# State copies behind the scans moved from ScalarE to VectorE in a Mamba-and-FFN block

## The reference

```python
mod = (_silu(c) @ wmod).reshape(1, 6, 1, -1)            # sa, ca, ga, sb, cb, gb
h = layernorm(x) * (1 + ca) + sa
# selective scan, D_INNER 1024, D_STATE 16
dt = softplus(dt_in @ dt_proj.T + bias);  dA = exp(dt * A);  dBx = dt * B * h
def step(hs, (dA_t, dBx_t, C_t)):  hs = dA_t * hs + dBx_t;  y = sum_n hs[., n] * C_t[n]
x = x + ga * (y + D * h)
h = layernorm(x) * (1 + cb) + sb
# FFN 1024 -> 2752 -> 1024, gate/up/down each with a rank-16 addition, silu(gate) * up
x = x + gb * ffn(h)
```

## Time and profile before

| | us |
|---|---|
| median of 3 runs | 2325.9 (2323.68 to 2330.59) |
| profiled execution | 2327.44 |
| its span, first to last instruction | 2325.6 |
| TensorE busy | 2064.8 |
| GpSimd busy | 1543.6 |
| VectorE busy | 1444.6 |
| ScalarE busy | 1061.0 |
| mean granted TensorE clock | 0.939 of full speed |

### The profile page before, as it was taken

One profiled execution on the slowest core, in us unless ns is written; L12 is line 12 of the kernel. 1 busy time (PEld: TensorE's weight loads), 2 busy tenths in 40 slices (PEclk: granted clock), 3 DMA queues, 4 the chain that ended last, 5 costly groups with the idle time before them and its releaser, 6 DMA issues.

```text
span 2325.6 us, 33254 instructions
## 1 busy us (share of the span) xinstructions
PE 2064.8 (89%) x11700; PEld 1875.5 (81%) x11700; DVE 1444.6 (62%) x2119; ACT 1061.0 (46%) x2378; POOL 1543.6 (66%) x960
## 2 busy tenths in 40 slices
PE   7577765878788999999999989999989999999999
PEld 4233324767777988888999989999889999999999
DVE  4664667667756778867778767778757774211111
ACT  3776766565535555544555444545444332310000
POOL 1477768997887797868877867867859896110100
PEclk9797867889888999999999999999999999999999
DMA  9799774777868677767577666677677877787786
GB/s 359 287 348 350 258 285 157 265 251 271 298 215 306 227 254 249 282 216 272 200 264 249 223 227 255 221 252 258 219 226 261 276 248 272 245 298 264 254 291 221
DMA packets 121205, 603.01 MB, mean 259 GB/s; under 512 B 10576, under 2 KB 23120, under 8 KB 80464
## 3 DMA queue, kind: packets, MB, share of 16 engines
q1 hardware_dynamic: 121040, 600.89, 73.4%
HBM read 514.63 MB, written 86.21 MB: 258 GB/s over the span
## 4 chain that ended last, share of the span: by engine, by line
PE 59%; DVE 14%; ACT 8%; issue 8%; POOL 6%; DMA 3%; DVEq 0%; ACTq 0%; SPq 0%; POOLq 0%
PE FP L759 50%; DVE ring L1162 6%; PE FP L647 4%; DVE ring L1047 3%; POOL ring L1276 2%; DVE FP L1137 2%; ACT SC L830 1%; ACT sqb L947 1%; PE FP L783 1%; DMA raw<-w_gu 1%; PE FP L720 1%; PE FP L676 1%; POOL y L1251 1%; DMA wts<-w_scratch 1%; POOL xlo L1267 1%
## 5 line engine op out<-in xcount | busy, mean ns | idle before, releaser
L759 PE MATMUL FP<-xhi,wts 128*128 128x368 f32 (+2 forms) x4320 | 1079.3, 326 | 76.8 <-issue 28.0
L759 PEld LDWEIGHTS FP<-xhi,wts 128*128 128x128 f32 x4320 | 774.8, 194 | 86.8 <-issue 78.3
L1276 POOL TENSOR_TENSOR ring<-ring,c_row 128x736 f32<-128x736 f32 (+2 forms) x372 | 621.2, 1670 | 295.6 <-ACT hst L847 295.1
L830 ACT ACTIVATE SC<-dtb,aneg 128x368 f32<-128x368 f32 (+2 forms) x768 | 412.1, 545 | 730.7 <-DVE ring L1162 729.5
L759 PE MATMUL FP<-xlo,wts 128*128 128x368 f32 (+2 forms) x2160 | 700.4, 324 | 0.0
L759 PE MATMUL FP<-hhi,wts 128*128 128x368 f32 (+5 forms) x2376 | 574.3, 323 | 39.8 <-POOL hlo L1291 22.9
L1162 DVE TENSOR_TENSOR_SCAN ring<-SC,hst,ring 128x368 f32<-128x368 f32 (+1 forms) x640 | 579.7, 947 | 3.1 <-ACT SC L830 3.1
L1251 POOL TENSOR_TENSOR y<-y,ring 128x736 f32<-128x736 f32 (+1 forms) x320 | 554.7, 1733 | 13.7
L759 PEld LDWEIGHTS FP<-hhi,wts 128*128 128x128 f32 (+1 forms) x2376 | 410.5, 187 | 47.0 <-POOL hlo L1291 23.6
L759 PEld LDWEIGHTS FP<-xlo,wts 128*128 128x128 f32 x2160 | 419.3, 194 | 1.1
L1047 DVE TENSOR_TENSOR ring<-hb,SC 128x736 f32<-128x736 f32 (+2 forms) x384 | 328.2, 855 | 102.2 <-PE FP L676 76.6
(11 more groups left out here) (102 smaller groups left out, 1966.9 us busy)
## 6 DMA issues: line engine op xcount, KB each, us to landing
wts<-w_scratch SPq DMA_DIRECT2D x249, 1152.0 KB, 5.3
wts<-w_scratch SPq DMA_DIRECT2D x91, 896.0 KB, 5.0
wts<-w_scratch SPq DMA_DIRECT2D x51, 1024.0 KB, 5.4
w_scratch<-wts SPq DMA_DIRECT2D x44, 1152.0 KB, 7.4
raw<-w_gu SPq DMA_DIRECT2D x44, 576.0 KB, 6.3
modw<-mod_w SPq DMA_DIRECT2D x24, 1024.0 KB, 11.0
w_scratch<-wts SPq DMA_DIRECT2D x16, 896.0 KB, 6.4
w_scratch<-wts SPq DMA_DIRECT2D x9, 1024.0 KB, 5.2
```

The source lines that it names most:

```text
L759: last = mm(out, w, x, start=(start and k == 0 and e == 0), stop=(stop and k == n - 1 and e == 2))
L830: A(decays(c, n, a), tile_of(dtb, c, i), ACT.Exp, scale=aneg[:, i * NS + s:i * NS + s + 1]).then_inc(a_da[a], 1)
L1276: G.tensor_tensor(buf, buf, over_pair(c_of(k)), ALU.mult).then_inc(g_hc, 1)
```

## The change

`keep_state` leaves ScalarE's list and stands in VectorE's, directly behind the two scans of the group, as a `tensor_copy` with the semaphore `v_save`. It waits for both scans. In the last chunk, whose states nobody reads, there is no copy, and GpSimd waits for the scans instead. The scans of a chunk's first pair wait for `v_save` where they waited for `a_save`.

```diff
--- before.py
+++ after.py
@@ -384,7 +384,7 @@
         a_xs, a_part, a_sp, a_fac = sem("xs_rounded"), sem("abs_ready"), sem("exp_ready"), sem("factor_ready")
         a_ini, a_keep = sem("h_times_d_ready"), sem("dt_kept")
         a_da = [sem(f"decay{a}_ready") for a in range(2)]
-        a_bc, a_save = sem("c_copied"), sem("state_kept")
+        a_bc, v_save = sem("c_copied"), sem("state_kept")
         a_hi, a_ts, a_th, a_hh = sem("weight_hi_ready"), sem("lora_rounded"), sem("tanh_ready"), sem("hidden_hi_ready")
 
         v_const, v_c, v_mod, v_modstep, v_late = sem("vector_const_ready"), sem("silu_c"), sem("mod_ready"), sem("mod_step"), sem("mod_cols_copied")
@@ -838,13 +838,6 @@
                 elif k >= C_FIRST:
                     act.wait_ge(g_hc, k - C_FIRST + 1)
                 A(c_of(k), SC[:, BC0 + k % 2, 0:CH[row_state(k)[0]]], ACT.Copy).then_inc(a_bc, 1)
-
-            def keep_state(c, n):
-                T = CH[c]
-                s, q = state_of(c, n)
-                for a in range(2):
-                    act.wait_ge(v_scan[a], group_id(c, n) + 1)
-                A(hst[:, s * ND + 2 * q:s * ND + 2 * q + 2], ring_of(c, n)[:, :, T - 1], ACT.Copy).then_inc(a_save, 1)
 
             def hi_part(u, hi, src):
                 w = raw_cols(u)
@@ -963,7 +956,6 @@
                             decay(0, n + 2)
                         elif n + 2 > GROUPS:
                             decay(1, 0)
-                        keep_state(0, n)
                         if n + 3 <= GROUPS:
                             copy_c(n + 3)
                     else:
@@ -971,7 +963,6 @@
                             copy_c(row_id(c, n) + 1)
                         if group_after(c, n):
                             decay(*group_after(c, n))
-                        keep_state(c, n)
 
             def split_hi(g):
                 k = OTF.index(g)
@@ -1045,6 +1036,12 @@
                 dve.wait_ge(pe_b, k + 1)
                 ring_free(dve, c, n)
                 V.tensor_tensor(ring_of(c, n), pair_of(hb, c, q), over_pair(SC[:, BC0 + k % 2, 0:T]), ALU.mult).then_inc(v_dbx, 1)
+
+            def keep_state(c, n):
+                s, q = state_of(c, n)
+                for a in range(2):
+                    dve.wait_ge(v_scan[a], group_id(c, n) + 1)
+                V.tensor_copy(hst[:, s * ND + 2 * q:s * ND + 2 * q + 2], ring_of(c, n)[:, :, CH[c] - 1]).then_inc(v_save, 1)
 
             def mod_vectors(n):
                 step = [{0: 0, 1: 1, 2: 5}[n]]
@@ -1152,7 +1149,7 @@
                         dbx(*group_after(c, n))
                     dve.wait_ge(v_dbx, g + 1)
                     if c and q == 0:
-                        dve.wait_ge(a_save, 3 * NS + s + 1 if c == 1 else group_id(c - 1, n) + PAIRS)
+                        dve.wait_ge(v_save, 3 * NS + s + 1 if c == 1 else group_id(c - 1, n) + PAIRS)
                     for a in range(2):
                         i = 2 * q + a
                         buf = ring_of(c, n)[:, a, :]
@@ -1161,6 +1158,8 @@
                             dve.wait_ge(a_da[1], g + 1)
                         V.tensor_tensor_scan(buf, decays(c, n, a), buf, hst[:, s * ND + i:s * ND + i + 1] if c else 0.0,
                                              ALU.mult, ALU.add).then_inc(v_scan[a], 1)
+                    if c + 1 < CHUNKS:
+                        keep_state(c, n)
                 elif kind == "evac":
                     q, T = p[1], CH[0]
                     dve.wait_ge(pe_y, NS * (q + 1))
@@ -1272,7 +1271,11 @@
                     if group_id(c, n) > GROUPS:
                         add(*divmod(group_id(c, n) - 1, GROUPS))
                     pool.wait_ge(a_bc, k + 1)
-                    pool.wait_ge(a_save, group_id(c, n) + 1)
+                    if c + 1 < CHUNKS:
+                        pool.wait_ge(v_save, group_id(c, n) + 1)
+                    else:
+                        for a in range(2):
+                            pool.wait_ge(v_scan[a], group_id(c, n) + 1)
                     G.tensor_tensor(buf, buf, over_pair(c_of(k)), ALU.mult).then_inc(g_hc, 1)
                     if not group_after(c, n):
                         add(c, n)
```

## The result

The changed kernel takes 2356.17 us (median of 6 runs, 2353.03 to 2359.1) against 2325.9: ratio 1.0129, 95% interval 1.0114 to 1.0145, so about 30 us slower, where 2354 had been forecast. The profiled execution took 2353.03 us, the shortest of the six, so the two profiles lie 25.6 us apart and not 30; its span is 2351.2, the mean granted clock 0.934 (0.939 before).

A forecast was written before the change was run, and what follows sets the result against it. TensorE was busy 2064.8 of 2325.6 us, so other engines matter only where it stands. Terms -8.0, -8.3, +11.5, +7.7 and +25 gave +28 us, 2354 us; own range 2328 to 2380 (58%), over all cases 2314 to 2390.

The forecast's parts named there:

- The deciding term: VectorE's copy behind the scans is held while GpSimd's instruction runs: 0.55 us left in the mean over 318 scan ends.
- ScalarE -8.0: Copies leaving ScalarE: 80 places on the chain at 0.10 us each, 8.0 us less.
- GpSimd -8.3: GpSimd's multiply by C starts earlier, after VectorE's copy: 15 places on the chain at 0.55 us, 8.3 us less.
- The unheld copy: VectorE's cost per copy when nothing blocks it: 0.03 us wait, 0.135 us copy, lost overlap; together 0.25 us.
- the first rival: The tiny VectorE copy isn't held by GpSimd: -2 us, 2324 us, no measurable change; chance 18%.
- The three positive terms: Losses in the sum: VectorE's 25 chain places +11.5, GpSimd's wait for the copy +7.7, copies off the chain +25 us.
- the term for the 25 places: Where the chain goes from a group's second scan to another VectorE instruction: 25 x (0.25 + 0.21) = +11.5 us.
- the coarse term for the other 143: Off the chain, 143 groups pushed by 0.79 us each, 112 us, times 0.225 = +25 us; ends 0 and 50.
- GpSimd's new wait: GpSimd, busy at the scans' end, then waits for a copy starting only when it pauses: 25 x 0.31 = +7.7 us.
- The coarse share: VectorE's time on the chain, 326 us of its 1444.6 us busy: 0.225, applied to delays off the chain.
- Place: Predicted profile sign: TensorE's lost time grows between 383 and 1645 us, its busy time doesn't.
- The third rival: VectorE's copy is passed over while GpSimd has a further instruction ready: +34 beside the +28 us, 2388 us; chance 10%.

The follow-up runs named there:

- Two pairs of kernels: tensor_copy against tensor_reduce on VectorE: in the changed kernel 1.0129 and 1.0002; as an additional instruction in the kernel before 1.0177 and 1.0051.
- the last chunk's edit: Kernel before, with ScalarE's copies left out in the last chunk alone, where GpSimd waits for the scans: 2326.25 us, ratio 0.9988.
- the reduce: Changed kernel with a tensor_reduce (max over one element) in place of each tensor_copy on VectorE: 2329.12 us, ratio to before 1.0002.
- the extra reduce: Kernel before, ScalarE's copies kept, plus a VectorE tensor_reduce into a spare buffer behind the scans, GpSimd waiting for both: 2338.15 us, 1.0051.
- the extra copy: Kernel before, ScalarE's copies kept, plus a VectorE tensor_copy into a spare buffer behind the scans, GpSimd waiting for both: 2369.41 us, 1.0177.
- only chunk 0: Changed kernel with VectorE's tensor_copy in chunk 0 alone, ScalarE's copies in chunks 1 to 4, none in the last: 2335.36 us, 1.0027.

## Why the prediction was right

- *The deciding term, a copy held for what remains of GpSimd's instruction.* It was read from two of five instructions at the start of the program that are 128 times as large. It held: mean 636 ns where 0.135 + 0.55 = 0.69 us had been worked out from GpSimd's state at 318 ends of scans, and 215 of 320 copies meet a running instruction where 227 of 318 had been counted. Two pairs of kernels that differ in the kind of instruction alone put 1.3% to the holding. That what GpSimd's instruction keeps for itself is a pair of SBUF ports is what the Trainium skill says (SBUF — State Buffer, Who interferes with whom); the runs show the holding, that two elements suffice and one doesn't, and that a reduce is free of it, not which part of the chip does it.
- *ScalarE -8.0 and GpSimd -8.3.* Together 16.3; without any copies it was 17 (12 to 21). The runs don't part the two. GpSimd's part is the less certain: with ScalarE's copy ahead of the second decay its waits fell by 31 us and no gain beyond that of the last chunk's edit is seen, though there the copy also delays the second decay, by 0.10 us after the step in the earlier trace rows.
- *The unheld copy.* 6 + 8 = 14 us had been put to it in the first rival; the reduce lies 1.0002 - 0.9928 = 0.7%, 17 us, above the kernel without copies, and the extra reduce 12 us above the kernel before. In detail the working was a little off: the copy starts 0.10 us behind the scans' end (1201.17 against 1201.07), not 0.03, and takes 0.17, not 0.135; the next starts 0.11 later. From the old start of the next (0.09 before the scans' end) that is 0.30 us, not 0.25.
- *The three positive terms.* +11.5, +7.7 and +25 are 44; measured is 2356 - 2314 = 42 by the medians and 1.0129 - 0.9928 = 2.0%, 47 us give or take 6, by the ratios, each of which compares within one set of runs. The sum is right, the parts aren't shown right: VectorE's copies stand 95 times in the chain with VectorE's next instruction behind, not 25 times, so the term for the 25 places was too small and the coarse term for the other 143 carried it. GpSimd's new wait, priced at 25 x 0.31, was too large: the 104 multiplies behind a copy of over 0.20 us waited 0.17 us in the median, and the chain passes from a copy to GpSimd 13 times, not 40. The coarse share (0.225 of VectorE's time) can be held against the two pairs: 29 us for 157 and 145 us of holding, all its effects together, are 0.19 and 0.20. That it lay so near, and that the other two errors cancelled, owes something to luck.
- *Place.* TensorE was to lose time between 383 and 1645 us. It does, 15 of the 25.6 us in the spans, but 10.6 are lost ahead of that, in a stretch for which I had priced places in the chain and named no loss. TensorE's busy time was to stay; it grew by 13 us. 7 of them lie before the first FFN, in the stretch of the first row (same columns), where the granted clock fell from 0.77 to 0.75 and 203 us busy became 211 with nearly the same instructions; no run here tells whether the longer gaps are the cause. The two other kernels with such copies in chunk 0 show 208 us there (the extra copy at 0.76, only chunk 0 at 0.77), the reduce 201 at 0.78. The row after:

```profile
75.00:383.00 308.00, 210.64 (x607) 100.89 (x607) 237.71 (x411) 206.44 (x441) 211.45 (x126) 0.75 0.78 284
```

- *The third rival,* GpSimd's queue going first, happens plainly in one of the 215 copies. VectorE, then GpSimd:

```profile
505.70 3.69 DVE L1044 COPY hst<-ring 128x2 f32<-128x2 f32 x1
```
```profile
504.60 1.76 POOL L1262 TENSOR_TENSOR y<-y,sqb 128x736 f32<-128x736 f32 x1
506.32 1.56 POOL L1250 TENSOR_TENSOR y<-y,ring 128x640 f32<-128x640 f32 x1
507.84 1.53 POOL L1279 TENSOR_TENSOR ring<-ring,c_row 128x640 f32<-128x640 f32 x1
```

The copy waits from 505.70 to 509.39, over the ends of two GpSimd instructions (506.36 and 507.88) that had a successor ready, and ends with the third at 509.37. It is rare here, probably because GpSimd's successor mostly waits for this very copy. A milder form is less rare: 16 copies started when the running instruction had under 0.07 us left and the next one started within 0.06 us of the copy's own start. These copies ended behind that next instruction, after 1.28 to 1.83 us, where the prediction had counted only what was left of the first.

## What to carry to other kernels

The price of a tiny instruction lies more in what it can be held by than in its size: here 29 us for being held and 12 to 17 us for standing there at all. So before moving one to VectorE look for an instruction of the same kind in the trace, compare its shortest with its longest time, and see what ends when the long ones end. In this kernel a copy on VectorE with source and target in SBUF and two fp32 elements per partition waited for GpSimd's running instruction; a `tensor_reduce` over one element did the same work in 0.16 us, two copies of one element in 0.15 us each. Larger copies, other types and other layouts were not tried. And a chain that counts such a copy as 0.10 us with "issue" behind it has to be read against the timeline.

## What the runs showed of the hardware that was not expected

- Holding begins at two elements: 128x1 copies took 142 to 157 ns in all of 640 cases, 128x2 copies 169 to 3689.
- A copy that meets a running GpSimd instruction ends 0.03 us behind that instruction's end, or after its own 0.17 us if that is later; 17 of 215 ended behind a later instruction's end, and one that started 0.01 us behind GpSimd's start wasn't held.
- A held copy can be passed over by GpSimd instructions that are ready, twice in the case above (3.69 us).
- GpSimd's own copy of 128x2 takes 189 ns, hardly more than VectorE's 170 and the same as the 188 that ScalarE's show in the median.
